# A loop on the engines or written-out steps: the middle of a 42-step software pipeline

## The reference, cut to what matters

```python
# layer 0: bottleneck with a deformable 3x3 convolution
out = relu(frozen_bn(conv2d(x, w1)))                 # 1x1, 1024 -> 256
offset = conv2d(out, w_off, pad=1, bias=b_off)       # 3x3, 256 -> 18
out = deform_conv3x3(out, offset, w2)                # 9 taps, bilinear samples, 256 -> 256
out = relu(frozen_bn(out))
out = frozen_bn(conv2d(out, w3))                     # 1x1, 256 -> 1024
x = relu(out + x)
# layer 1: masked grouped bottleneck, 4 groups
out = relu(gconv(x * mask, w1, 0)) * mask            # 1x1
out = relu(gconv(out, w2, 1)) * mask                 # 3x3
x = relu(gconv(out, w3, 0) + x)                      # 1x1
```

## Time and profile before

| | us |
|---|---|
| median of 3 timed executions | 2921.44 |
| lowest, highest | 2916.69, 2928.83 |
| the profiled execution, its time | 2910.46 |
| its span, first to last instruction | 2908.6 |
| PE busy | 2777.0 (95%) |
| DVE busy | 2280.3 (78%) |
| POOL busy | 1267.6 (44%) |
| ACT busy | 1226.3 (42%) |
| mean granted TensorE clock | 0.986 |
| mean data rate of the DMA engines | 297 GB/s |

### The profile page before, as it was taken

One profiled execution on the slowest core, in us unless ns is written; L12 is line 12 of the kernel. 1 busy time (PEld: TensorE's weight loads), 2 busy tenths in 40 slices (PEclk: granted clock), 3 DMA queues, 4 the chain that ended last, 5 costly groups with the idle time before them and its releaser, 6 DMA issues.

```text
span 2908.6 us, 46509 instructions
## 1 busy us (share of the span) xinstructions
PE 2777.0 (95%) x12960; PEld 1528.6 (53%) x12960; DVE 2280.3 (78%) x5216; ACT 1226.3 (42%) x2466; POOL 1267.6 (44%) x1159
## 2 busy tenths in 40 slices
PE   7978999999999999999999999999999999999998
PEld 3435555555545545555555555545555555555552
DVE  2138888887878888788887878888888888888871
ACT  1124444444444444344444444444444444444442
POOL 2035544544434534444443444534444455555530
PEclk9989999999999999999999999999999999999999
DMA  8779988888888889888888888989888888888862
GB/s 276 222 272 339 326 285 321 322 324 298 313 297 282 328 297 332 276 299 300 303 324 301 311 295 280 329 297 332 310 311 291 299 320 318 312 298 318 321 235 80
DMA packets 263148, 864.68 MB, mean 297 GB/s; under 512 B 31746, under 2 KB 72834, under 8 KB 254336
## 3 DMA queue, kind: packets, MB, share of 16 engines
q0 software_dynamic: 165888, 604.05, 58.7%
q1 hardware_dynamic: 78592, 190.68, 19.0%
q10 hardware_dynamic: 18432, 67.12, 5.7%
HBM read 747.72 MB, written 114.02 MB: 296 GB/s over the span
## 4 chain that ended last, share of the span: by engine, by line
PE 89%; DVE 5%; issue 3%; DMA 1%; ACT 1%; POOL 1%; DVEq 0%; SPq 0%; ACTq 0%; POOLq 0%
PE psA L422 14%; PE psR L533 14%; PE psD L513 9%; PE psD L514 9%; PE psD L515 9%; PE psR L565 9%; PE psV L494 9%; PE psR L582 4%; PE psR L546 4%; PE psA L461 3%; PE psR L588 3%; DVE val L951 2%; DVE y L934 1%; PE psD L461 1%; PE psA L441 1%
## 5 line engine op out<-in xcount | busy, mean ns | idle before, releaser
L387 POOL DMA_INDIRECT corners<-corner_tables,samples_in x1152 | 1252.6, 1087 | 1541.3 <-DVE val L951 1094.2
L951 DVE SCALAR_TENSOR_TENSOR val<-corners,samples_in,val 128x256 f32<-128x256 f32 x3456 | 1416.4, 477 | 84.1 <-issue 48.3
L715 ACT ACTIVATE valT_hi<-psV 128x512 fp32r<-128x512 f32 x576 | 311.7, 592 | 959.6 <-PE psD L515 763.4
L961 DVE TENSOR_TENSOR valT_lo<-psV,valT_hi 128x512 fp32r<-128x512 f32 x576 | 370.0, 684 | 247.8 <-ACT valT_hi L715 247.5
L701 ACT ACTIVATE val<-corners,samples_in 128x256 f32<-128x256 f32 x1152 | 490.4, 503 | 34.5 <-DMA corners<-corner_tables,samples_in 30.4
L513 PE MATMUL psD<-valT_hi,w_hi 128*128 128x512 f32 x1152 | 484.6, 421 | 0.4 <-DVE valT_lo L961 0.4
L533 PE MATMUL psR<-deformed,w_sb 128*128 128x512 f32 x1024 | 465.0, 596 | 12.5 <-DVE y L882 10.4
L514 PE MATMUL psD<-valT_hi,w_lo 128*128 128x512 f32 x1152 | 456.8, 397 | 0.0
L515 PE MATMUL psD<-valT_lo,w_hi 128*128 128x512 f32 x1152 | 455.8, 396 | 0.0
L422 PE MATMUL psA<-x_sb,w_sb 128*128 128x512 f32 x768 | 372.3, 626 | 33.7 <-DVE scratch L850 7.8
L494 PEld LDWEIGHTS psV<-const_sb,val 128*128 128x128 f32 x2304 | 261.2, 142 | 192.1 <-issue 118.5
(11 more groups left out here) (72 smaller groups left out, 1452.0 us busy)
## 6 DMA issues: line engine op xcount, KB each, us to landing
y<-in_x SPq DMA_DIRECT2D x128, 512.0 KB, 4.0
out<-y ACTq DMA_DIRECT2D x128, 512.0 KB, 3.2
x_sb<-in_x SPq DMA_DIRECT2D x48, 1024.0 KB
corner_tables<-x_sb SPq DMA_DIRECT2D x128, 256.0 KB, 4.9
corners<-corner_tables,samples_in POOLq DMA_INDIRECT x1152, 6.1
y<-in_x SPq DMA_DIRECT2D x8, 2048.0 KB, 10.9
corner_tables<-corners SPq DMA_DIRECT2D x8, 1139.0 KB, 8.6
samples_dram<-samples SPq DMA_DIRECT2D x32, 90.0 KB, 8.3
```

The costliest lines, as they stand in the source:

```text
L387: nc.gpsimd.indirect_dma_start(corners[:, slot, :], None, table, bass.IndirectOffsetOnAxis(ap=index[:, TAPS * t + k:TAPS * t + k + 1], axi ...
L715: nc.scalar.activation(valT_hi[:, m, :], psV[m][:], ACT.Copy).then_inc(valT_ready, 1)
L951: nc.vector.scalar_tensor_tensor(acc, corners[:, n % GS, corner * CMID:(corner + 1) * CMID], samples_in[:, bpar, w:w + 1], acc, ALU.mult, ...
L961: nc.vector.tensor_tensor(valT_lo[:, m, :], psV[m][:], valT_hi[:, m, :].bitcast(F32), ALU.subtract).then_inc(valT_rest, 1)
```

## The change

pipeline no longer builds loops. It calls step once for each of the 42 steps, with s as a number, s % 2 as parity, the stages that are on in this step, and low = s. The five step functions aren't touched. The order of the instructions that compute, of the DMAs and of the waits is the same on every engine; waits and addresses hold constants where they held registers computed from the loop's counter. Twenty more steps are written out than before.

```diff
@@ def pipeline(eng, step)
                       "C": (LAG_C, NB + LAG_C), "E": (LAG_E, NB + LAG_E),
                       "after T": (LAG_T + 1, NB + LAG_T + 1), "next B": (LAG_B, NB + LAG_B - 1)}
 
-            peeled = {0, LAG_B - 2, LAG_B, LAG_E, NB - 2, NB, NB + LAG_B - 2, NB + LAG_B}
-            s, last = 0, NB + LAG_E
-            while s < last:
-                end = s + 2
-                while s not in peeled and end < last and end not in peeled:
-                    end += 2
-                on = [{k for k, (a, b) in ranges.items() if a <= s + par < b} for par in range(2)]
-                if end - s > 2:
-                    with eng.Fori(s // 2, end // 2) as pair:
-                        for par in range(2):
-                            step(2 * pair + par, par, on[par], s + par)
-                else:
-                    for par in range(2):
-                        step(s + par, par, on[par], s + par)
-                s = end
+            for s in range(NB + LAG_E):
+                step(s, s % 2, {k for k, (a, b) in ranges.items() if a <= s < b}, s)
```

## The result

| | before | after |
|---|---|---|
| median of the timed executions, us | 2922.02 (4) | 2849.15 (4) |
| lowest, highest, us | 2916.69, 2928.83 | 2845.63, 2852.32 |
| the profiled execution, its time, us | 2910.46 | 2852.32 |
| its span, us | 2908.6 | 2850.5 |
| PE busy, us | 2777.0 | 2755.5 |

The changed kernel takes 0.9756 of the time before, 95% interval 0.974 to 0.9771. Beside the other experiments it was run again and gave 0.9765 (0.9741 to 0.979): 2850.24 against 2918.68. One execution in the slower state, 4393.42 us at a mean clock of 0.603, of the kernel before once more, is left out of the ratios. The forecast was 2861, within 2844 to 2882. The lines of the changed file are 13 lower than before's from pipeline on: conv1 is line 409, DVE's corners are 938, the grouped convolutions 533 and 552.

The account below looks back on a forecast made before the run. TensorE was taken to set the pace (chain 89% PE), with stops at loop back edges on the path. 53.1 + 1.8 + 4.7 = 59.6 us off the 2921.44 us median gave 2861.8, taken as 2861; range 2844 to 2882.

Parts of the forecast that it names:

- (1): Loop over steps 12 to 29: its eight back edges go, 6.6 us an edge, 53.1 us gained.
- (2): Same loop: register work for waits and addresses goes, 0.10 us a step over 18 steps, 1.8 us gained.
- (3): Loop over steps 34 to 37: its one back edge, where ACT stood, goes; 4.7 us gained.
- (4): Loop over steps 2 to 5: its one back edge gains nothing, at most 6.6 us.
- (5): Code of 20 more written-out steps must be brought in: cost zero, bounds minus 1.7 to 20 us.
- (a): Rival: stops return in the new straight code, 6.6 us each; one every two steps gives 2948 us; chance 0.03.
- (b): Rival: a few shorter stops in straight code lose a third to two thirds of the gain, 2881 to 2901; chance 0.06.
- (c): Rival: gathers set the pace and catch up at edges; mean tick stays 87.4 us, time about 2921; chance 0.02.
- (d): Rival: the loss belongs to the step boundary, not the branch, and stays; time 2921; chance under 0.01.
- (6): Full steps without stops: PE busy 83.52 of 83.84 us, nothing else uncovered, no wait added.
- The low alternative, 2851: Total if the 11 us between profiled execution and timed median were longer stops at the edges and go too.
- ACT none near 2500: Sign named in advance: in the tail near 2500 us ACT has no "issue" wait.

Follow-up runs that it names:

- the kernel before once more: Only a tuple's order edited against the kernel before, for a second profiled execution (2918.83 us); median 2915.09 us, ratio 0.9998.
- turns of six: Kernel before with the middle loop's turn six steps instead of two, 2 back edges instead of 8, all engines looped; 2871.45 us, ratio 0.9832.
- the padded loops: Kernel before with 250, 120 or 60 semaphore increments more a step in DVE's warm-up loop; pause behind its branch 3.45, 2.92 and 0.27 us.

## Why the prediction was right, point by point

(1) and (2), the middle: forecast 53.1 + 1.8 = 54.9 us. The profiles' 15 ticks lost 54.6; term (2) counted 18 steps of 0.1 us and these are 15, so 0.3 more lie outside them and the sum is 54.9. The mechanism is shown from several sides: it goes with the jump back (turns of six), the whole gain needs both PE and DVE written out, and those two suffice. What the mechanism is inside, code that has to be brought in again, fits the padded loops, but no run saw the engine waiting for the bytes.

PE's and DVE's losses lying side by side was argued from one edge. It held: 45.0 and 63.0 alone, 54.6 and 57.8 together. That DVE's stops with PE running free are dearer than both was not foreseen. One reading behind it was wrong: of DVE's eight waits for "issue" only seven are at back edges of the middle loop. The eighth middle edge is the one near 1724, whose 5.98 us stand under ACT's name, and the eighth wait is at the tail's back edge:

```profile
2540.00 3.26 DVE L951 SCALAR_TENSOR_TENSOR val<-corners,samples_in,val 128x256 f32<-128x256 f32 x8 [3.70 <-issue]
```

That the count came to eight was luck. The term is untouched by it, as it was taken from the ticks.

(3), the tail: forecast 4.7 us, measured 6.3 between the two profiles, 12.1 between the second profile of before and the changed kernel's, and 9 by the timed executions with the tail alone written out. Behind a looped middle this term was too small; behind a written-out middle the same loop cost 1.8 us. Its edge was ACT's, as forecast: DVE stood there too, but with DVE written out the tick over it was still 76.98 us. I gave the tick of 74.56 us to nothing, as it had no back edge in it. The runs show that it belonged to the loops all the same: in the tail's looped steps PE pauses 1.86 us before line 546 in place of 1.78, and then its matmuls in some steps take 5.35 us in place of 3.65. That was seen in one such step of before, three of the second profile, and in none of steps 33 to 38 where these were written out: in both profiles of the changed kernel, with the tail alone and with ACT written out as well. The pause goes with ACT's loop: it stays 1.86 with PE, with DVE or with both written out, and is 1.78 as soon as ACT is. But it isn't enough for the slow matmuls: with PE, with DVE, with both, or with the whole middle written out, all four looped steps have 1.86 us and none has slow matmuls; in every profile with all engines' loops left in middle and tail at least one step has them. What decides is open, and that the 0.08 us have a part in it is an inference.

(4), the warm-up: forecast nothing, and DVE goes on 0.27 us behind its branch there. The start differs by up to 5 us among profiles with and without loops.

(5), the added code: forecast zero between -1.7 and +20. The 20 new steps show no tick over 83.75 or 72.87 us. Rivals (a) and (b) are out: no stop in straight code reached the path. (c) is out: the mean tick is 83.74 at a DMA share of 0.88, and (d) with it.

(6): right, PE is busy 83.43 of 83.75 us.

The total: 59.6 us forecast, from the profile. The profiled executions differ by 58.1 (2850.9 forecast, 2852.32 measured): the middle gained 54.9 and the tail 6.3, and the start lost 2.65. So near a hit is in part luck, as 1.6 too little in the tail met the start's loss. The medians differ by 72.9 at first and 68.4 in the later set. The step that failed was the last, where I left the 11 us between before's profile and its median standing with "nothing ties them to the edges". The second profile ties such a difference to the loops: of its extra 8.4 us over the first, 3.2 are in the middle's 15 ticks, beside longer stops of DVE, and 5.9 in the tail's five, while the start is 0.7 earlier. It is one execution; the slower timed ones have no profile. The low alternative, 2851, was the better one. Of the signs named in advance, "ACT none near 2500" was badly put: the changed profile names "issue" for many of ACT's waits, and in those of 4.05 us before line 721 the idle time is what before had under DVE's name. The label isn't steady even for the same kernel: the second profile of before has 90.1 us of waits before line 734 under "issue", the first has none. The idle time has to be compared, not the label.

The Trainium skill (Runtime: NRT & Kernel Launch, "Instruction fetch mechanics") is borne out in its rule, that a jump back outside the buffered window stops the engine and straight code doesn't: 6.0 to 6.6 us against none. Its figures of 512 instructions for the other engines and 2048 for TensorE do not tell by themselves how long a turn may be. DVE stopped with a turn of 296 and TensorE with turns of some 1750 at seven of eight edges, while ACT went on with turns of 311. The section has the buffer made of two blocks, so the place of a turn in the blocks may matter; no run here varied it.

## What to carry to other kernels

When an engine's loop has a long turn, look at the tick over each back edge: a stop on one or more engines, once per jump, is the sign (mostly with no releaser, though one of the eight here stood under another engine's name), and what the tick over the edge has above the others, times the number of jumps back, is the gain from writing the steps out or from putting more steps into a turn. Stops of several engines at the same edge lie side by side, so all engines that stop must be freed together; freeing one can lose a little (TensorE alone, ratio 1.0022) or gain a part (VectorE alone, 0.9914). Price a loop's stretch from more than one profiled execution, and give it the slow-clock stretches that follow its pauses.

## What the runs showed that I had not expected

- The jump's price did not grow with the turn: 6.0 us with six steps in it, 6.6 with two.
- In the warm-up loop DVE went on with a turn of 176 instructions and stopped with one of 296. ACT went straight on behind its middle turns of 311 in every profile (0.2 us) and stopped 6.96 and 6.25 us with turns of 895. Its tail turn of 286 stopped in the kernel before (6.92 us from the branch to the new turn) and not with turns of six (0.21) or with the middle written out (0.25). TensorE's middle turns, some 1750 long, stopped at seven of eight edges of before (branch of 3.54 to 5.79 us, 0.23 at the eighth), its tail turn of 1457 never. Length alone doesn't decide; the rest is open.
- Freeing TensorE alone made the kernel 0.2% slower: it reached DVE's stop earlier, waited 4.74 us at the first edge and then ran eight matmuls in 5.29 us. DVE's stops were also longer there, 55.0 us in all.
